# An mLSTM + MLP kernel on one core: the state update as four 32-column matmuls in place of one 128-column matmul, and the carried weights split before the fourth stack

## The reference, cut to what matters

```python
xn = _layernorm(x)                       # x is 8 x 1024 x 512, float32
x = x + attn(xn) + ffn(xn)               # ffn: silu gate, hidden size 2048

def step(carry, xs):                     # attn: mLSTM scan, 8 heads, q and k of 32, v of 64
    C, n, m = carry
    ...
    C_new = F[..., None, None] * C + (I[..., None] * k_t)[..., :, None] * v_t[..., None, :]
    n_new = F[..., None] * n + I[..., None] * k_t
    h_num = jnp.einsum('bhd,bhdv->bhv', qs, C_new)
    ...
```

## Time and profile before

| | |
|---|---|
| median of 3 runs | 3163.22 us (3162.7 to 3164.44) |
| time of the profiled execution | 3165.01 us |
| its span, first to last instruction | 3163.3 us |
| mean granted TensorE clock | 0.999 of 2.4 GHz |
| TensorE matmul busy | 3067.6 us, 97% of the span |
| VectorE busy | 1925.3 us, 61% |
| ScalarE and GpSimd busy | 1121.3 us (35%) and 771.3 us (24%) |

### The profile page before, as it was taken

One profiled execution on the slowest core, in us unless ns is written; L12 is line 12 of the kernel. 1 busy time (PEld: TensorE's weight loads), 2 busy tenths in 40 slices (PEclk: granted clock), 3 DMA queues, 4 the chain that ended last, 5 costly groups with the idle time before them and its releaser, 6 DMA issues.

```text
span 3163.3 us, 61615 instructions
## 1 busy us (share of the span) xinstructions
PE 3067.6 (97%) x22426; PEld 2234.5 (71%) x22426; DVE 1925.3 (61%) x4371; ACT 1121.3 (35%) x2142; POOL 771.3 (24%) x1127
## 2 busy tenths in 40 slices
PE   0899999999999999999999999999999999999999
PEld 0677777777777777777777777777777777777776
DVE  8666556666566565566565566665566665665655
ACT  5433333333333333333333233333333333333332
POOL 5321222222222222222222222212222222222222
PEclk9999999999999999999999999999999999999999
DMA  5000000000000000000000000000000000000000
GB/s 220 8 14 13 7 7 13 13 13 13 7 7 13 13 13 13 7 7 13 13 13 13 0 13 13 13 13 7 7 13 13 13 13 7 7 13 13 13 13 7
DMA packets 20333, 51.08 MB, mean 16 GB/s; under 512 B 1506, under 2 KB 1634, under 8 KB 18274
## 3 DMA queue, kind: packets, MB, share of 16 engines
q1 hardware_dynamic: 20322, 50.95, 4.3%
HBM read 34.16 MB, written 16.78 MB: 16 GB/s over the span
## 4 chain that ended last, share of the span: by engine, by line
PE 79%; DVE 13%; issue 4%; ACT 3%; POOL 0%; DMA 0%; ACTq 0%; SPq 0%; DVEq 0%
PE work L1042 17%; PE work L1041 17%; PE work L1040 17%; PE acc L1042 6%; PE acc L1041 6%; PE acc L1040 6%; DVE arena L866 3%; DVE arena L865 3%; PE o_bank L1128 3%; PE o_bank L1187 2%; PE work L1193 2%; DVE arena L913 2%; DVE arena L916 1%; ACT arena L640 1%; DVE amax L707 1%
## 5 line engine op out<-in xcount | busy, mean ns | idle before, releaser
L1040 PE MATMUL work<-xt,weights 128*128 128x256 f16 x4608 | 1257.3, 273 | 0.0
L1041 PE MATMUL work<-xt,weights 128*128 128x256 f16 x4608 | 1257.2, 273 | 0.0
L1042 PE MATMUL work<-xt,weights 128*128 128x256 f16 x4608 | 1257.2, 273 | 0.0
L540 POOL TENSOR_TENSOR arena<-arena 128x256 f16<-128x256 f32 x512 | 348.5, 681 | 1728.6 <-ACT arena L650 1728.6
L913 DVE SCALAR_TENSOR_TENSOR arena<-arena,work 128x256 f32<-128x256 f32 x512 | 215.1, 420 | 539.4 <-ACT arena L646 536.3
L1040 PEld LDWEIGHTS work<-xt,weights 128*128 128x128 f16 x4608 | 479.1, 104 | 69.7
L1041 PEld LDWEIGHTS work<-xt,weights 128*128 128x128 f16 x4608 | 451.4, 98 | 70.0
L1042 PEld LDWEIGHTS work<-xt,weights 128*128 128x128 f16 x4608 | 451.3, 98 | 52.6
L646 ACT ACTIVATE arena<-work,unscale 128x256 f32<-128x256 f32 x512 | 241.1, 471 | 588.3 <-PE work L1042 587.9
L650 ACT ACTIVATE arena<-arena 128x256 f16<-128x256 f32 x512 | 213.3, 417 | 598.9 <-DVE arena L916 598.9
L1040 PE MATMUL acc<-weights,arena 128*128 128x512 f16 x1024 | 388.1, 379 | 0.0
(11 more groups left out here) (193 smaller groups left out, 4036.9 us busy)
## 6 DMA issues: line engine op xcount, KB each, us to landing
arena<-x_dram SPq DMA_DIRECT2D x33, 512.0 KB, 3.4
out_dram<-arena SPq DMA_DIRECT2D x32, 512.0 KB, 2.8
weights<-w_g_dram SPq DMA_DIRECT2D x4, 1024.0 KB, 13.0
weights<-w_u_dram SPq DMA_DIRECT2D x4, 1024.0 KB, 20.6
arena<-w_d_dram SPq DMA_DIRECT2D x4, 1024.0 KB, 26.3
arena<-w_qk_dram SPq DMA_DIRECT2D x1, 1024.0 KB, 6.2
arena<-w_v_dram SPq DMA_DIRECT2D x1, 1024.0 KB, 8.2
weights<-w_o_dram SPq DMA_DIRECT2D x1, 1024.0 KB, 17.4
```

Source lines behind the costliest of these rows:

```text
L540: g.tensor_tensor(hh[:, j % HB, 1, :], tt[:, j % 2, :], hh[:, j % HB, 0, :], ALU.subtract).then_inc(h_ready, 1)
L1040: t.matmul(dst, w[0], a[0], start=first, stop=False, skip_group_check=True)
L1041: t.matmul(dst, w[0], a[1], start=False, stop=False, skip_group_check=True)
L1042: return t.matmul(dst, w[1], a[0], start=False, stop=last, skip_group_check=True)
```

## The change

The 128-column matmul of a state update becomes four, one per head: 32 columns of weights (the head's keys), 66 columns of its own v, and an output on the head's own 32 partitions of the bank. The built program gives the four a tile of 128 rows by 32 columns of the array at columns 0, 32, 64 and 96; all other matmuls of the loop have the full 128 x 128 array, except those of line 1152, which have 64 rows x 128 columns. VectorE no longer masks: four instructions of 32 partitions by 66 columns update the four diagonal blocks of the state straight from PSUM. `own_head` and its five fills on GpSimd go. Some semaphore waits change their name: what waited for `state_ready` waits for the bank of the update two units before. In `AFTER[3]`, `wT` comes before `stack3`.

```diff
-AFTER[3] = ["stack3", "wT"]
+AFTER[3] = ["wT", "stack3"]
...
-            link(g.memset(own_head[:, :], 0.0))
-            for h in range(HG):
-                link(g.memset(own_head[h * DQ:(h + 1) * DQ, h * VW:(h + 1) * VW], 1.0))
...
-                            d.tensor_tensor(upd, own_head[:, :], bank(f"st{k_}")[:, 0:GW],
-                                            ALU.mult).then_inc(free_of(f"st{k_}"), 1)
-                            wait_drained(dve, i, f"st{k_}")
-                            d.scalar_tensor_tensor(out=state[:, g, :], in0=state[:, g, :],
-                                                   scalar=decay[:, g, c:c + 1], in1=upd, op0=ALU.mult,
-                                                   op1=ALU.add).then_inc(state_ready, 1)
+                            if c:
+                                wait_drained(dve, i, f"st{k_ - NG}")
+                            for h in range(HG):
+                                rows, cols = slice(h * DQ, (h + 1) * DQ), slice(h * VW, (h + 1) * VW)
+                                ins = d.scalar_tensor_tensor(out=state[rows, g, cols], in0=state[rows, g, cols],
+                                                             scalar=decay[rows, g, c:c + 1],
+                                                             in1=bank(f"st{k_}")[rows, 0:VW], op0=ALU.mult,
+                                                             op1=ALU.add)
+                            ins.then_inc(free_of(f"st{k_}"), 1)
                             if k_ == 3:
 
-                                dve.wait_ge(state_ready, START + i * 5 + 4)
+                                wait_drained(dve, i, "st2")
+                                wait_drained(dve, i, "st3")
...
-                            pe.wait_ge(state_ready, START + i * 5 + (k - 1 if c else 0))
+                            if c:
+                                wait_drained(pe, i, f"st{k - NG}")
+                            else:
+                                pe.wait_ge(state_ready, START + i)
...
-                            t.matmul(bank(f"st{k}")[:, 0:GW], kt[:, c, g * P:(g + 1) * P],
-                                     v[:, c, g * HG:(g + 1) * HG, :], start=True,
-                                     stop=True).then_inc(work_full, 1)
+                            for h in range(HG):
+                                rows = slice(h * DQ, (h + 1) * DQ)
+                                mm_ = t.matmul(bank(f"st{k}")[rows, 0:VW],
+                                               kt[:, c, g * P + h * DQ:g * P + (h + 1) * DQ],
+                                               v[:, c, g * HG + h, :], start=True, stop=True)
+                            mm_.then_inc(work_full, 1)
```

More of the change, by code:

```diff
@@ L188, in mlstm_mlp_kernel @@
         diag = sb("diag", [P, NH], F32)
-        own_head = sb("own_head", [P, GW], F32)
         restart = sb("restart", [NH, BLOCK], F32)
@@ L220, in mlstm_mlp_kernel @@
                  ("v", NCH * NH * VW), ("to", 512), ("pm", 1024), ("lf", 256), ("ip", 256), ("bc", 256),
-                 ("mm", 256), ("upd", GW), ("num", NH * VW),
+                 ("mm", 256), ("spare", GW), ("num", NH * VW),
                  ("hof", 512), ("hoh", 512), ("kp", 512), ("tt", 512), ("hh", 768), ("res", 1024),
@@ L268, in mlstm_mlp_kernel @@
         state = at["state"].rearrange("p (g n) -> p g n", g=NG)
-        upd = at["upd"]
         num = at["num"].rearrange("p (h e) -> p h e", h=NH)
```

## The result

The changed kernel takes 3150.30 us (3150.09 to 3150.36, 6 runs) against 3163.77 us (3162.70 to 3164.44, 6 runs): a ratio of 0.9957, 95% interval 0.9945 to 0.9970. It is 13.5 us faster. The forecast was 3188 us, with a range of 3148 to 3215 and a chance of 0.26 for faster. The measured time lies in the range, but only at its low end, which had been stretched down for rivals 1 and 2. Two executions fell far outside (4007 us of the kernel before, at a granted clock of 0.763, and 12891 us in experiment 7), and no ratio counts them.

A forecast was written before the change was run, and what follows sets the result against it. TensorE's own stream bounds the kernel (matmuls 97% of the span). Strips cost 0.12 + 0.19 + 0.415 − 0.445 = +0.28 per unit, x 128 = +35.8 us, less 10.8 gained: +25.0, so 3188 us, range 3148 to 3215.

The forecast's parts named there:

- first rival: At the strips: tile shape changes along columns cost nothing, so 3142 to 3154 us, faster; chance 0.2.
- second rival: At the strips: emptying as forecast, but strips run wholly side by side, so 3149 us, faster; chance 0.07.
- The moved split: TensorE's wait at line 1152 for VectorE's line 932 goes: 9.0 us in 31 blocks, 1.2 in the first, together 10.2.
- Ahead of the loop: Without GpSimd's `own_head` fills the next piece of the weights' split starts 1.2 earlier; bounds 0 and 1.2, 0.6 us taken.
- (a): Way into the strips, per unit: 0.09 of emptying and 0.03 for an uncovered 32-column load, together 0.12 us.
- (b): Way back, per unit: 0.09 emptying plus exposed load, 0.11 float32 (`pv0` to `pv2`) or 0.06 float16 (`pv3`); mean 0.19.
- (c): The update's eight 66-column passes per unit: 0.46 one after another, 0.37 to 0.40 overlapping; 0.415 us taken, lowest bound 0.11.
- VectorE: Its four 66-column state instructions take 0.22 each, 0.9 per unit in all, hidden beside TensorE's `ffn`; nothing in the sum.

The follow-up runs named there:

- experiment 7: Changed kernel with the two matmuls behind the split over all 128 rows of the array, zeros from row 40 on: 3139.92 us, ratio 0.9924.
- Experiment 1: Kernel before with only the order in `AFTER[3]` changed, `wT` before `stack3`; update still one masked 128-column matmul: 3153.21 us, ratio 0.9967.
- experiment 3: Changed kernel with the update as one full-array 128-column matmul again, VectorE still taking the four diagonal blocks without mask: 3152.73 us, ratio 0.9965.
- experiment 8: Changed kernel with all updates of a block in one stretch of sixteen strip matmuls behind `pv1`, ScalarE copy, second state buffer: 3121.31 us, ratio 0.9866.
- Experiment 4: Changed kernel with the four small matmuls all in one strip, the first 32 columns of the array: 3192.74 us, ratio 1.0093.
- experiment 5: Changed kernel with one head's matmul per update instead of four, VectorE still doing all four: 3148.20 us, ratio 0.9949.

## Why the prediction was wrong, point by point

- **The moved split** was right: 9.0 us from 31 blocks was worked out from an emptying of 0.09, and the start after the last `acc` matmul came out at 0.31, as 0.22 + 0.09 says. The traces give 0.294 per block, 9.1 in 31. Experiment 1 gives 10.1 for all 32 blocks against 10.2. That the total fits so well is in part luck: the first block gave 0.6 up to its next `ffn`, not 1.2, since the prediction left out line 916 there, and the median leaves open how much of the clock's 1.7 is in it. The 1.8 that the prediction took from its profiled execution to the median is of the size of this fall of the clock, which it did not know of.
- **Ahead of the loop** 0.6 was taken, and experiment 3 against 1 gives 0.5, none of it from VectorE's part. Right in size. The piece of the weights' split that was to start 1.2 earlier starts at 41.99 in the changed kernel, 0.9 earlier, and then has waited 0.68 for ScalarE.
- **(a) and (b), the changes of tile shape**, were right for the longer case: 0.09 and 0.02 on the way in (0.12 forecast), 0.09 and 0.10 on the way out (0.20). The first rival, that a change along columns costs nothing, falls: the emptying is there in each unit, and experiment 8 gained 29.0 by having three round trips fewer per block. Behind `pv3`, the float16 load shows far less than the 0.06 I had: the matmul behind the update starts at 1021.95 and the next at 1022.18, 0.01 more than an undisturbed 0.22. That is why the strips gain behind `pv3` and not elsewhere.
- **(c), the eight passes, is the step that failed.** The prediction took 0.415, "the middle of 0.37 and 0.46", and called 0.11 the lowest bound; measured are 0.13, hardly more than that bound. Two of its reasons were wrong. It held that the next head needs 0.03 for its load before it can start: the first four passes start within 0.02 of each other, for loads into different strips overlap too. And it took the nearest row, one of passes that share the array, as if it spoke for strips. Experiment 4 shows where that number does hold: in one strip the passes take 0.33 more, and the kernel lands at 3192.7, 5 us from the forecast 3188. The error, 0.415 − 0.13 = 0.28 per unit, x 128 = 36 us, is nearly the whole 38 between 3188 and 3150.
- **The second rival was what happened**: emptying as forecast, strips wholly side by side, 3149 us; it had a chance of 0.07. The page TensorEngine Tiling (Array Packing) of the Trainium skill gives, in its section Overview, up to four times the speed for a stationary side of 32 columns. The runs agree for the passes themselves: 0.13 for eight, 0.46 one after another in one strip, a factor of 3.5. The same page of the Trainium skill says in its section Tiling Modes that a change of the mode drains the array. The runs agree with that too: 0.09 at each change. I gave weight to the second statement and nearly none to the first.
- **VectorE** was mis-sized and harmless: 0.28 each for the 0.22 taken, 1.16 per unit for 0.9, all hidden, as the equal blocks of experiments 1 and 3 show.

The strips therefore moved little in sum. In `pv0` to `pv2` they save 0.31 (0.445 to 0.13) and pay as much around them; in `pv3` they pay about 0.22. Over 128 units this is 2.4 us.

## What to carry to other kernels

Small matmuls in column strips cost here what one strip's share costs, but going in and out of the strips costs about 0.3 us when a float32 load of 128 columns follows. So gather all strip work of a block in one place (29.0 us here). The one unit with a float16 matmul behind its strips pays 0.09 less, so such a neighbour should be the better one; no run moved one there. Look also for places that have a narrow tile without need: filling 40 rows up to 128 with zeros was worth more here (10.4 us) than the strips (2.4). And where an order of steps is set by hand, look whether what the bound engine waits for can stand before what it doesn't need yet; this one line was three quarters of the gain. Last, look at the granted clock of the profiled execution stretch by stretch before reckoning from it: the mean of 0.999 hid a stretch at half the clock that cost 1.7 us.

## What the runs showed of the hardware that I had not expected

- Four loads and four passes of different strips start 0.007 apart, and each strip's second pass begins 0.08 behind its first, 0.02 of which are the wait for the first load. In experiment 8, 32 passes in four strips lasted 0.67 by their records, the same as 8 passes in one strip (0.65): each strip takes its own passes one after another, and the four do not disturb each other.
- Behind the strips, a float16 load of 128 columns holds its matmul back by about 0.01, a float32 one by 0.10.
- The list of waits puts part of the emptying down to a data wait of the weight loads ("PEld work L1197 <- DVE arena L911: 11.0" in 32 blocks) although that engine had finished (in the `pv3` shown above, line 911 ended at 1021.52 and the load starts at 1021.69); experiments 4 and 5 have the same entry with the same 11.0.
